# Per-batch products in 64x32 tiles and two rows of x per run, in a kernel that adds two chosen linear maps to x

## The reference

```python
x = x + einsum('bct,bcd->bdt', x, W0[subject])      # 8 matrices
x = x + einsum('bct,bcd->bdt', x, W1[condition])    # 200 matrices
```

## Time and profile before

| | us |
|---|---|
| median of three runs | 103.44 |
| the three runs | 103.44, 108.72, 102.52 |
| span of the profiled execution (first to last instruction) | 100.5 |
| TensorE busy in that span | 80.8 |
| VectorE, ScalarE, GpSimd busy | 35.6, 26.7, 31.6 |

### The profile page before, as it was taken

One profiled execution on the slowest core, in us unless ns is written; L12 is line 12 of the kernel. 1 busy time (PEld: TensorE's weight loads), 2 busy tenths in 40 slices (PEclk: granted clock), 3 DMA queues, 4 the chain that ended last, 5 costly groups with the idle time before them and its releaser, 6 DMA issues.

```text
span 100.5 us, 1338 instructions
## 1 busy us (share of the span) xinstructions
PE 80.8 (80%) x324; PEld 47.2 (47%) x324; DVE 35.6 (35%) x37; ACT 26.7 (27%) x33; POOL 31.6 (31%) x136
## 2 busy tenths in 40 slices
PE   0003089994999999999999999998999999999500
PEld 0001078994944574484366448443734844444100
DVE  4205714582252424405142441514242242441300
ACT  5000003454224141242424124142304424124400
POOL 2400028782037782004768200076175000000000
PEclk9999999999999999999999999999999999999975
DMA  2899999999999999999999999999999974678975
GB/s 13 240 426 450 374 385 389 388 384 388 390 384 389 389 383 389 387 385 389 386 393 405 408 409 404 404 409 408 407 409 386 391 292 159 249 277 309 347 281 206
DMA packets 17333, 35.83 MB, mean 357 GB/s; under 512 B 689, under 2 KB 818, under 8 KB 17202
## 3 DMA queue, kind: packets, MB, share of 16 engines
q1 hardware_dynamic: 17186, 33.69, 90.3%
q0 software_dynamic: 144, 2.10, 4.9%
HBM read 19.01 MB, written 16.78 MB: 356 GB/s over the span
## 4 chain that ended last, share of the span: by engine, by line
PE 72%; DMA 10%; POOLq 3%; POOL 3%; issue 2%; DVE 2%; SPq 1%; ACT 1%
PE psum L227 48%; PE psum L210 14%; DMA w_rows<-in_L_cond_weights_dram,cond 9%; PE psum L202 9%; POOLq L164 3%; POOL w0t_diag L169 3%; DVE w L261 1%; ACT xy L278 1%; DMA subjects<-in_itok_B_dram 1%; POOLq L169 1%; SPq L119 0%; SPq L110 0%; SPq L116 0%; DVE w_rows L311 0%
## 5 line engine op out<-in xcount | busy, mean ns | idle before, releaser
L227 PE MATMUL psum<-xy,m_diag 128*128 128x512 f32 (+1 forms) x128 | 56.8, 598 | 0.0
L169 POOL COPY w0t_diag<-w0t 64x64 f32 x128 | 29.7, 232 | 42.9 <-issue 35.8
L227 PEld LDWEIGHTS psum<-xy,m_diag 128*128 128x128 f32 x128 | 23.4, 190 | 28.0 <-issue 26.5
L278 DVE COPY xy<-psum 128x1024 f32<-128x1024 f32 (+1 forms) x16 | 19.6, 1225 | 27.9 <-PE psum L227 27.9
L278 ACT COPY xy<-psum 128x1024 f32<-128x1024 f32 (+1 forms) x16 | 16.2, 1012 | 42.5 <-PE psum L227 42.5
L210 PEld LDWEIGHTS psum<-w,w0t_diag 128*128 128x128 f32 x128 | 15.2, 192 | 5.1 <-issue 3.4
L210 PE MATMUL psum<-w,w0t_diag 128*128 (+1 forms) x128 | 15.2, 273 | 1.7 <-DVE w L261 1.3
L202 PE MATMUL psum<-ident,w_rows 128*64 128x128 f32 x64 | 9.7, 330 | 4.6 <-DVE w_rows L311 4.6
L272 DVE COPY m_diag<-psum 64x512 f32<-64x512 f32 x8 | 5.5, 683 | 17.8 <-PE psum L210 17.8
L202 PEld LDWEIGHTS psum<-ident,w_rows 128*64 128x64 f32 x64 | 8.7, 161 | 5.9 <-DVE w_rows L311 5.0
L261 ACT COPY w<-psum 64x512 f32<-64x512 f32 x8 | 4.6, 578 | 17.2 <-PE psum L202 17.1
(11 more groups left out here) (6 smaller groups left out, 0.7 us busy)
## 6 DMA issues: line engine op xcount, KB each, us to landing
xy<-in_x_dram SPq DMA_DIRECT2D x16, 1024.0 KB, 11.0
out_dram<-xy SPq DMA_DIRECT2D x16, 1024.0 KB, 9.8
w_rows<-in_L_cond_weights_dram SPq DMA_DIRECT2D x1, 128.0 KB, 5.5
cond<-in_itok_B_dram SPq DMA_DIRECT2D x1, 0.5 KB, 2.1
subjects<-in_itok_B_dram SPq DMA_DIRECT2D x1, 0.5 KB
w_rows<-in_L_cond_weights_dram,cond POOLq DMA_INDIRECT x1, 9.4
```

What stands on the lines that cost most here:

```text
L169: nc.gpsimd.tensor_copy(w0t_diag[rows, r, n // 2, h * C:(h + 1) * C], w0t[rows, bass.ds(picked[n] * C, C)]).then_inc(s_w0_diag, 1)
L227: last = nc.tensor.matmul(y_psum[:, slot, k, :], m_diag[:, r, t * TILE + k, :], xy[:, pair, :].rearrange("q o t -> q (o t)"), start=True, ...
L278: copy(xy[:, bass.ds(i * ITER + (r * GROUP + t * TILE), TILE), :], y_psum[:, slot, :, :]).then_inc(done, 1)
```

## The change

- x lies in SBUF as slots of four batches: partition 32 b + p holds channels 2p and 2p+1 of batch b, side by side. A contiguous run in DRAM is then two rows, 4 KB. A unit is two slots, eight batches; there are 16 units and 32 slots.
- M is computed per batch, from the plain turned W0 (`w0b`, no block-diagonal tile, so no clearing of it): for each of the two channel parities j one matmul with a 64x32 stationary tile and 64 moving columns, 16 matmuls per unit. VectorE and ScalarE spread M into the new `m_diag` by multiplying with a mask of zeros and ones.
- A slot is applied by four matmuls with 64 rows of contraction: two halves of the partitions h, each accumulating over the two parities j, into two banks. Unit 0 has a form of its own (`apply_single`), with 32x64 tiles, unmasked copies of M and stores in runs of 2 KB.
- The results are copied as four pieces of 64x512 per slot, two on VectorE and two on ScalarE (unit 0: one of 128x512 on each).
- `cond` is loaded as one row, converted to fp32, turned into a column by a TensorE transpose, and copied back as integers before the gather.
- Only 1.5 MB of x is loaded before the gather; SP waits with the rest until VectorE has written the first 16 pieces of `w0b`. GpSimd writes the other 112. All other loads are issued without waits between them.
- W0 and the subjects are loaded by ScalarE. ScalarE then makes 18 copies, and behind each of them TensorE does three transposes whose result nobody reads.
- The W1 transposes are copied in turns of four, with two copies of 64x256 for each turn.
- ScalarE issues the stores of units 0 to 3, SP those of units 4 to 15; the last unit is stored slot by slot, 0.5 MB each.
- All loops are unrolled.

```diff
-    x_view = x_dram.rearrange("(p h) c t -> (h c) p t", h=2)
-    out_view = out_dram.rearrange("(p h) c t -> (h c) p t", h=2)
+    x_view = x_dram.rearrange("(s b) (p j) t -> (b p) s (j t)", b=SLOT, j=J)
+    single_out_view = out_dram.rearrange("(s r) c t -> s c r t", r=SLOT)
+    out_view = out_dram.rearrange("(s b) (q i) t -> (b q) s (i t)", b=SLOT, i=J)
...
+    BLOCKS = [(0, 1), (1, 1)] + [(v, 2) for v in range(2, UNITS, 2)]
+    SINGLE = 1; M_COLUMNS = 4; M_RING = 8; M_BANKS = [6, 4] + [6] * 7; Y_RING = 3
+    TURN = 4; W1_RING = 6; EARLY = 2; TICKS = 18; LATER = 4; WARM = 3
...
+        def store(eng, s, n):
+            eng.wait_ge(s_y_v, 2 * (s + n))
+            eng.wait_ge(s_y_s, 2 * (s + n))
+            if s < 2 * SINGLE:
+                for odd, rows in enumerate(HALVES):
+                    eng.dma_start(single_out_view[s + odd], ...).then_inc(s_out[s // 2], 16)
+            else:
+                eng.dma_start(out_view[:, s:s + n, :], xy[:, s:s + n, :]).then_inc(s_out[s // 2], 16)
...
+            sp.dma_start(cond_row[:, :], cond_dram.rearrange("(o b) -> o b", o=1)).then_inc(s_cond_row, 16)
+            load(0, 2)
+            load(2, 1)
+            sp.wait_ge(s_w0b_early, EARLY * UNIT)
+            load(3, 1)
+            for v in range(2, UNITS):
+                load(2 * v, 2)
+            for v in range(LATER, UNITS - 1):
+                store(sp, 2 * v, 2)
+            store(sp, SLOTS - 2, 1)
+            store(sp, SLOTS - 1, 1)
...
+            nc.tensor.transpose(cond_psum, cond_float[:, :], ident[0:1, 0:1]).then_inc(s_cond_turned, 1)
...
+            for n in range(TICKS):
+                pe.wait_ge(s_tick, n + 1)
+                for z in range(WARM):
+                    nc.tensor.transpose(psum[0:C, z, 0:P], w0_rows[:, z, :], ident[:, :])
...
+            def products(k):
+                first, n = BLOCKS[k]
+                ...
+                for v in range(first, first + n):
+                    for j in range(J):
+                        for r in range(SLOT):
+                            for odd, rows in enumerate(HALVES):
+                                at = (v % M_COLUMNS * J + j) * C
+                                last = nc.tensor.matmul(psum[QUARTERS[r], M_BANKS[k] + odd, at:at + C],
+                                                        w0b[rows, v * SLOT + r, j * Q:(j + 1) * Q],
+                                                        w1[rows, v * SLOT + r, :], start=True, stop=True)
+            def apply(k):
+                ...
+                for s in range(2 * first, 2 * (first + n)):
+                    v, odd = s // 2, s % 2
+                    pe.wait_ge(s_x[v], 32 if v == 1 else 16)
+                    if s >= Y_RING:
+                        pe.wait_ge(s_y_v, 2 * (s - Y_RING + 1))
+                        pe.wait_ge(s_y_s, 2 * (s - Y_RING + 1))
+                    for j in range(J):
+                        for h, rows in enumerate(HALVES):
+                            last = nc.tensor.matmul(psum[:, 2 * (s % Y_RING) + h, :],
+                                                    m_diag[rows, odd, v % M_RING, j, :],
+                                                    xy[rows, s, j * T:(j + 1) * T],
+                                                    start=j == 0, stop=j == J - 1)
+            def apply_single(k):
+                ...
+                for half in range(2):
+                    s = 2 * v + half
+                    for j in range(J):
+                        for h in range(2):
+                            rows = QUARTERS[2 * half + h]
+                            for odd, columns in enumerate(HALVES):
+                                last = nc.tensor.matmul(psum[columns, 2 * (s % Y_RING) + h, :],
+                                                        m_diag[rows, odd, v, j, 0:C],
+                                                        xy[rows, 2 * v + odd, j * T:(j + 1) * T],
+                                                        start=j == 0, stop=j == J - 1)
+            products(0)
+            for k in range(len(BLOCKS)):
+                if k + 1 < len(BLOCKS):
+                    products(k + 1)
+                if BLOCKS[k][0] < SINGLE:
+                    apply_single(k)
+                else:
+                    apply(k)
...
+        def copies(eng, copy, scale, w1_done, m_done, y_done, odd):
+            for n in range(odd, TURNS, 2):
+                copy_w1(eng, copy, w1_done, n)
+            eng.wait_ge(s_mask, 2 * SLOT)
+            copy_m_single(eng, copy, m_done, odd, 0)
+            copy_m(eng, scale, m_done, odd, 1)
+            for k, (first, n) in enumerate(BLOCKS):
+                for s in range(2 * first, 2 * (first + n)):
+                    ...
+                        copy_y(eng, copy, y_done, odd, s)
+                    if odd and s % 2 == 0 and 0 < s <= 2 * LATER:
+                        store(nc.scalar, s - 2, 2)
+                if k + 2 < len(BLOCKS):
+                    copy_m(eng, scale, m_done, odd, k + 2)
```

More of the change, by code:

```diff
@@ L106, in _ @@
         @block.sync
         def _(sp):
[L108 to L128, removed]
@@ L131, in _ @@
[L131 to L142, removed]
@@ L146, in _ @@
+            for v in range(LATER, UNITS - 1):
+                store(sp, 2 * v, 2)
+            store(sp, SLOTS - 2, 1)
+            store(sp, SLOTS - 1, 1)
+            for v in range(UNITS):
+                sp.wait_ge(s_out[v], 32 if v < SINGLE or v == UNITS - 1 else 16)
         @block.gpsimd
@@ L156, in _ @@
                 in_=w1_dram.rearrange("s d e -> s (d e)"),
[L157 to L173, removed]
-            pool.wait_ge(s_subjects, 16)
[L175 to L181, removed]
+                in_offset=bass.IndirectOffsetOnAxis(ap=cond[:, 0:1], axis=0)).then_inc(s_gather, 16)
+            pool.wait_ge(s_subjects, 16)
+            for first in range(EARLY * UNIT, B, 2 * UNIT):
+                _, picked = nc.values_load_multi_w_load_instructions(
+                    subjects[0:1, first:first + 2 * UNIT], engines=(POOL,), min_val=0, max_val=S0 - 1,
+                    skip_runtime_bounds_check_because="subjects index the 8 matrices")
+                if first == EARLY * UNIT:
+                    pool.wait_ge(s_gather, 16)
+                    pool.wait_ge(s_w0t, 4)
+                for n in range(2 * UNIT):
+                    v, odd, r = (first + n) // UNIT, n // SLOT % 2, n % SLOT
+                    nc.gpsimd.tensor_copy(w0b[HALVES[odd], v * SLOT + r, :],
+                                          w0t[HALVES[odd], bass.ds(picked[n] * C, C)]).then_inc(s_w0b, 1)
         @block.tensor
@@ L207, in products @@
[L207 to L212, removed]
-                last.then_inc(s_m_psum, 1)
[L215 to L229, removed]
-                    last.then_inc(s_y_psum, 1)
@@ L245, in _ @@
-            products(0, 0)
-            group(0, 0)
-            group(0, 1)
-            with pe.Fori(1, TURNS - 1) as i:
-                group(i, 0)
-                group(i, 1)
-            group(TURNS - 1, 0)
-            group(TURNS - 1, 1, following=False)
+            for n in range(TURNS):
+                if n >= W1_RING:
+                    before = n - W1_RING
+                    pe.wait_ge((s_w1_v, s_w1_s)[before % 2], 2 * (before // 2 + 1))
+                for z in range(TURN):
+                    last = nc.tensor.transpose(psum[0:C, n % W1_RING, z * B:(z + 1) * B],
+                                               w1_rows[:, :, n * TURN + z], ident[:, :])
+                last.then_inc(s_w1_turned, 1)
@@ L263, in copy_w1 @@
-            last.then_inc(done, 1)
-        def copy_m(eng, copy, done, h, i, r):
-            eng.wait_ge(s_m_psum, i * RING + (r + 1))
-            before = i * (RING * TILES) + (r - 1) * TILES
-            if not (isinstance(before, int) and before <= 0):
-                eng.wait_ge(s_y_psum, before)
-            copy(m_diag[HALVES[h], r, :, h * C:(h + 1) * C], m_psum[HALVES[h], r, :, :]).then_inc(done, 1)
-        def copy_y(eng, copy, done, slot, i, r):
-            for t in range(slot, TILES, RING):
-                eng.wait_ge(s_y_psum, i * (RING * TILES) + (r * TILES + t + 1))
-                copy(xy[:, bass.ds(i * ITER + (r * GROUP + t * TILE), TILE), :],
-                     y_psum[:, slot, :, :]).then_inc(done, 1)
@@ new lines, in copy_w1, with copy_m_single @@
+            for odd, rows in enumerate(HALVES):
+                copy(w1[rows, :, n * TURN:(n + 1) * TURN].rearrange("q (v r) k -> q v r k", r=SLOT),
+                     turned[:, odd, :, :, :]).then_inc(done, 1)
+        def copy_m_single(eng, copy, done, odd, k):
+            v = BLOCKS[k][0]
+            eng.wait_ge(s_m_psum, k + 1)
+            copy(m_diag[:, odd, v, :, 0:C], psum[:, M_BANKS[k] + odd, v * J * C:(v + 1) * J * C].rearrange(
+                "q (j e) -> q j e", j=J)).then_inc(done, 2)
@@ L295, in _ @@
         @block.vector
         def _(dve):
```

(22 more changed lines are left out.)

178 lines of the change are left out of this document (101 added, 77 removed).

## The result

The changed kernel takes 92.91 us (median of 6 runs, 92.64 to 93.06) against 102.59 (median of 6): ratio 0.907, 95% interval 0.903 to 0.911. In a second session it was 92.85 against 102.04, ratio 0.910 (0.906 to 0.914). The ratios leave out the executions that ran some per cent longer at a lower granted clock, such as the one of 108.72 us before. The forecast was 100.2, with a range from 95.5: the direction was right, the size was not.

What follows compares the result with a forecast made beforehand. TensorE was taken as the bound: first apply at 22.6 us (27.6 less 0.4, 2.5, 0.5, 1.55), plus 70.0 gives 92.6, plus tail 4.9 is 97.5, plus 2.9 is 100.4, rounded to 100.2; range 95.5 to 107.5.

Steps and rivals of the forecast that it cites:

- The bound of the kernel before: Whole kernel: TensorE, busy 80.8 of 100.5 us, sets the end; transfers are close behind but do not.
- Start of the gather, W1: Before the products: gather lands net 0.4 us earlier, W1 transposes at full clock save 2.5, smaller last copies 0.5.
- the cond detour: Before the gather: a VectorE copy, a TensorE record and another VectorE copy add 0.5 us, bounds 0.3 and 1.2.
- Products: TensorE's matmuls that compute M: 512 records at 0.032 us each, bounds 0.013 and 0.112, in place of 128 at 0.112.
- Apply: TensorE's matmuls on x: two halves run side by side, 1.72 us per slot, 55.2 for 32 slots.
- Order in TensorE: Rival, chance 0.22, no change: strict start order makes unit 0 take 6.9 us, not 3.45; time 103.7.
- The drain: Part of the order rival: array empties at each of 16 tiling changes, 0.35 us each, 5.6 in all; time 105.8.
- Tail: Behind TensorE's end: last copies cost 0.4 us more, the halved last store saves 1.6; 4.9 in place of 6.1.
- Transfers: All loads and stores: 35.8 MB need until 91 us at 407 GB/s, just under TensorE's end; no gain, no loss.
- the rival of fuller overlap: Products at 0.013 us lose 9.7 more, then transfers and VectorE bound the end; chance 0.18, faster, time 95.5.
- the 2.9 us around the span: Whole kernel: median time lies 2.9 us above the profiled span, the lowest run 2.0; added to the sum.
- ScalarE's stores: Rival, chance 0.08, no change: ScalarE's store issues wait behind SP's loads, 0.8 us lost in each of four units; 103.4.

Runs made afterwards that it cites:

- b_few_products: Kernel before, but from group 3 on only one of the eight products of a group issued; 97.56 us, ratio 0.952.
- string (5): Part of e_tiles: apply matmuls four in a row on one half of the rows, then four on the other, twice; took 8.6 us.
- a_twice: Changed kernel with every product issued twice, 512 records more; 101.56 us, ratio 0.996.
- a_no_ticks: Changed kernel without the 18 ScalarE copies and the 54 idle transposes behind them; 95.04 us, ratio 0.932.
- a_no_hold: Changed kernel without SP's wait for VectorE's pieces of w0b, all x loads issued at once; 94.45 us, ratio 0.922.
- e_tiles: Changed kernel with strings of repeated product and apply matmuls on chosen tiles behind the last copy; one execution, product records 10 to 57 ns apart.

## Why the prediction was right or wrong

**The bound of the kernel before**: right, and b_few_products adds how near the next one was: 4.8 us below.

**Start of the gather, W1**: predicted landing 12.2, measured 12.60, within the bounds; the cond detour cost nothing beside the 3.19 of the earlier trace rows (the gather was issued at 3.09), but the smaller share of x beside the gather gained nothing either. The W1 transposes started 0.109 apart from the second on, the last at 19.85: as forecast. Products began at 21.02, 0.5 later than the sum implied (22.6 less two strings of products, 20.55), and 0.4 of it is the gather. VectorE's two copies per turn, 0.42 each and 0.03 between, take 0.90 for two turns of TensorE, which are 0.87: they ran end to end and would have set the pace had TensorE been any faster. That bound I had not priced.

**Products**: this step failed, and with it the time. I scaled the present spacing with the weight columns, 0.107 x 32/128 + 0.005 = 0.032, as if weight loads stood in one line. They do not: 0.010 per record inside a string, 0.0123 with the changes around it. Over 512 records that is 10 us, and TensorE's end was 82.5, not 92.6 (1.4 less in unit 0 and 1.2 more in the other slots nearly cancel). The value lay even under my lower bound of 0.013. "Nearest row" was no guide here: the present record has the whole array for itself, so no row could show whether two tiles load at once.

**Apply**: 1.77 per slot for a predicted 1.72; the records of the two halves start 7 ns apart. Right.

**Order in TensorE**: unit 0 was neither 6.9 nor 3.45 but 2.0, for its 32 records use eight tiles of 32x64, where I had counted four. Eight records start between 22.035 and 22.117, and eight tiles are in use only if the second half's first records are among them, ahead of twelve records that precede them in the program. The rule of "TensorE: Matmul & The Clock Gate" of the Trainium skill, Part 3, that matmuls start and end in program order, is not what this trace shows. The limit seen in string (5) fits, for in unit 0 no tile has more than four records. **The drain** of "TensorEngine Tiling (Array Packing)" of the Trainium skill, Key Properties, would be a loss of time at each change, and there is one, but small: a block of 7.86 us holds 6.87 of apply and 0.64 of products, which leaves 0.35 for two changes, 2.8 us in all where I priced 5.6. That the array empties in that time no run shows.

**Tail**: 4.9 predicted; 5.05 where TensorE sets the end (a_twice, a_no_ticks), 8.4 in the changed kernel. The step was right for a kernel bound by TensorE; its condition failed with the products. The slack of 8.4 - 5.05 = 3.35 us accounts for the spans: TensorE's end later by 4.0 (a_no_hold), 4.6 (a_no_ticks) and 12.3 (a_twice) gave 1.0, 1.2 and 8.9, where the slack says 0.7, 1.3 and 8.9.

**Transfers**: the second step that failed. I said that the transfers bring no gain and no loss, which holds only while TensorE is the bound; by my own sum they were just under it, so a shorter TensorE had to run into them. They took back 3.35 of what TensorE gained. Priced at 407 GB/s where 409 to 418 came, they made the rival of fuller overlap 95.5 when 92.9 was measured. The remainder of that gap is the 2.9 us around the span: it was 1.75 (the profiled execution took 92.65 with a span of 90.9); the lowest run of before, with 2.0, had pointed that way. The sum's 100.4 was also written down as 100.2.

**ScalarE's stores**: its issues took 0.38 to 0.69 us while SP's took up to 3.5 in the same stretch (26.9 to 39.1 us). ScalarE does not wait for SP's full queue; that rival is out.

**Where the gain comes from**: with runs of 2 KB the changed kernel's span is 94.2 to 94.9 instead of 100.5, the floor of such runs; the longer runs lower that floor to 90.9. So TensorE's shortening pays about 6 us without them, and they add 3.4. Of the 11.9 us that TensorE lost, 3.35 are unused.

## What to carry to other kernels

When a change makes the bounding engine much faster, work out the next floor with the same care as the first, for it gives the result: here bytes over the rate at the new run length. An unknown price that multiplies hundreds of instructions deserves its mechanism's real bounds, not a scaled row. With two bounds 3.35 us apart, a delay near the start is free only while it stays within that slack and leaves the transfers busy: a small load queued behind a large one cost 3.0 us, through one of them or both.

## What the runs showed of the hardware

- A string of fp32 records of 64 columns: 57 ns apart on one 64x32 tile, 28 on two, 14 on four, 10 on eight.
- Packets of 4 KB took 159 ns, those of 2 KB 84 to 86, and the 16 KB packets of the gather 611 (medians of the transfer records). Stretches in which they dominate flowed at 409 to 418 GB/s, 387 to 407 and 427.
- A record may start ahead of earlier ones of another tile: twelve in unit 0, three in string (5) of e_tiles. Both fit a limit of four records of one tile ahead of the next tile's; that limit is my estimate from these starts.
- A change between 64x32 and larger tiles cost 0.13 us (e_tiles) to 0.18 (changed kernel).
- In the middle of product strings TensorE stood still for 1.3 to 2.5 us, three times in a_twice and once in a_no_ticks, each time beside a 16 KB packet of the instruction queue. Other such packets passed without a gap (26.25 in the changed kernel), so that it waited for instructions is a reading, not shown.
